# Mixture-of-experts blocks in two parts, with routing, scatter, gather and norm of one part beside the blocks of the other

## The chip, the cores and the metric

The kernel runs on one core of a Trainium2 chip. Its engines run at the same time and meet by semaphores: TensorE (PE; PEld is its weight load), VectorE (DVE), ScalarE (ACT), GpSimd (POOL) and SyncE (SP). The metric is the device time of one execution in microseconds (us), as the median of the runs.

## The reference

The input x is 4 x 1024 x 128 (four batches). Two layers follow each other, each with an attention and a mixture of experts:

```python
for layer in (0, 1):
    sa, ca, ga, sb, cb, gb = mod(c)                  # six vectors of 128 per batch
    h = layernorm(x) * (1 + ca) + sa
    x = x + ga * attention(h)      # layer 0: 16 heads, window 64; layer 1: 16 heads of 8, full
    h = layernorm(x) * (1 + cb) + sb
    x = x + gb * experts(h)
# experts, layer 0 (F = 512; layer 1: F = 256, no biases, tanh gelu, and a small
# attention across the four batches before it)
    xn = layernorm(h) * gamma + beta
    probs = softmax(xn @ Wg.T + bg)                  # 8 experts, for each of 4096 tokens
    w = the two largest of probs (layer 0: over their sum), else 0
    y_e = gelu(xn @ W1[e].T + b1[e]) @ W2[e].T + b2[e]
    out = h + sum_e w[:, e] * y_e
```

Every token thus needs two of eight experts.

## The kernel before

**Stages.** The program is a row of stages, each an `nc.Block` with one instruction list for every engine. At the end of a stage all engines drain and meet, so a stage begins when the slowest engine has ended the last one. Within a stage each list is run in its written order.

**Tiles.** x lies in SBUF as 32 tiles of 128 tokens (NT), 8 to a batch (TPB), and is handled in 8 chunks of 4 tiles (CPT, NCH). K.nat holds the modulated h, K.x the residual stream. `K.mod_rows` holds the modulation vectors on every partition.

**Routing** (class `RoutedExperts`, M). For each batch TensorE makes the logits, and VectorE and ScalarE the softmax and the two choices. `place` gives each token and choice a row number in a DRAM buffer `moe_rows`, a region of 4096 rows for each expert (SPAN = B·T), by a running count over the batches. GpSimd then scatters each normalised tile twice by an indirect DMA, 64 in a layer (`scatter_one`, L1413; `scatter`, L1402). `tabulate` (VectorE, L1378 to L1394) turns the counts into a table: for each of NBK = 39 blocks of 256 rows (2·4096/256 + 8 - 1) its expert and its first row. 39 always suffice, since each of the eight experts fills at most one block in part; the others take spare rows.

**Layer 0's order.** The window attention routes batches 0 to 2 beside its own work, one batch behind. `route_last_stage` (L1102) takes batch 3: both norms, logits, choice, place, table, and on GpSimd the 32 scatters of batches 2 and 3. Then `block_stage` with name moe0b, then `gather_qkv_stage` (L1682), which gathers the experts' rows, sums them into x, and makes norm and q, k, v of layer 1's attention. The attention (its first product L2021) starts behind it.

**Layer 1's order.** `last_norm_stage` (L292, L316) normalises and routes all four batches and scatters 64 times; then `block_stage` as moe1b, then `gather_stage` (L1602), which ends the program with the output stores.

**Block stage** (L1454). For block j SP loads the 256 rows (xin, 6 buffers) and the expert's weights (wblock, 6 buffers). TensorE turns block j+1 (`turn`, xps), makes the hidden layer of block j (hps) and the output rows of block j-1 (yps). VectorE copies xps to xT with the affine (L1556), and yps to y (L1566 with bias, L1568 without). ScalarE issues the store of block j-3 back into `moe_rows` (L1528) and does the gelu (L1542). xps and yps have two PSUM banks each. VectorE adds gb·h to x by two instructions for a chunk (L1578, L1580, `residual`) in blocks 2 to 9. GpSimd only clears operands of the coming attention in layer 0 (L1879), and has nothing in layer 1.

```python
                    if j + 1 < NBK:
                        turn(j + 1)
                    if j < NBK:
                        hidden(j)
                    if j >= 1:
                        out_rows(j - 1)
```

**Gather.** GpSimd gathers two rows for each token, 64 indirect DMAs of a tile each (L1687, L1606). When a chunk's 8 gathers are in, it is multiplied by the first weight (ScalarE in layer 0, L1749; VectorE in layer 1), and VectorE does a fused multiply and add for each tile (L1787), the gate, and the sum into x (L1795). In layer 0, GpSimd's norm step (`deviation`, L145) of a batch stands between the gathers.

## Time and profile before

| | us |
|---|---|
| median of 3 runs | 2082.85 |
| lowest and highest | 2081.83, 2082.87 |
| the profiled execution | 2078.63 |
| its span in the trace | 2076.9 |
| route_last_stage, from the end of the window attention to the first load of the blocks | 617.1 to 679.4 |
| block stage moe0b | 679.4 to 837 |
| gather_qkv_stage up to attention's first product | 837.3 to 957.3 |
| last_norm_stage up to the first load of the blocks | 1784.9 to 1898.3 |
| block stage moe1b | 1898.3 to 1988 |
| gather_stage | 1988.4 to 2076.9 |

TensorE is busy 76% of the span, VectorE 64%, ScalarE 55% and GpSimd 26%. These shares are averages over stages with different limits, so they are read by stretch of the program. The trace gives each instruction's start and length, the time for which its engine was idle before it, and what released it. An engine with a q behind it (SPq, PEq) stands for its queue: DMA issues, drains, branches. The granted clock is TensorE's, 1.00 being 2.4 GHz and 0.50 being 1.2 GHz.

### The profile page before, as it was taken

Reading aid. Unit: us, or ns where it says so; the run is one execution under the profiler, and the core shown is the slowest. Engines: PE = TensorE matmul, PEld = TensorE weight load, DVE = VectorE, ACT = ScalarE, POOL = GpSimd, SP = SyncE. Lnnn points to the kernel's source line nnn. Section 1 sums busy time; section 2 is a strip of 40 time slices with the busy share of each in tenths; the row PEclk is TensorE's granted clock in tenths of the full one; section 3 lists DMA queues with packets and bytes.
Section 4 is the critical chain, followed back from the end, with each engine's and each line's share of the span. In section 5 each row is a group of like instructions: output and inputs, shape, how many; then the busy total and the mean of one; then the engine's idle time right before and its main releaser. Section 6 shows DMA issues by size and latency. Waiting matters only on the chain. (4 is left out here: it accounts for less than half of the span.)

```text
span 2076.9 us, 34430 instructions
## 1 busy us (share of the span) xinstructions
PE 1575.3 (76%) x11512; PEld 915.2 (44%) x11512; DVE 1338.5 (64%) x3318; ACT 1135.4 (55%) x2965; POOL 550.0 (26%) x615
## 2 busy tenths in 40 slices
...
GB/s 189 42 162 157 103 28 35 45 31 40 40 21 41 230 226 183 57 134 63 20 26 18 26 18 26 20 24 25 19 18 2 1 4 0 13 52 123 255 86 73
DMA packets 86203, 138.99 MB, mean 67 GB/s; under 512 B 18084, under 2 KB 57252, under 8 KB 85900
## 3 DMA queue, kind: packets, MB, share of 16 engines
...
## 5 line engine op out<-in xcount | busy, mean ns | idle before, releaser
L2130 DVE TENSOR_REDUCE q_max<-s_ps 128x1 f32<-128x1024 f32 x512 | 597.9, 1217 | 14.6 <-PE s_ps L2021 7.0
L2111 ACT ACTIVATE probs<-s_ps 128x512 f32<-128x512 f32 x1024 | 535.5, 602 | 124.8 <-PE s_ps L2042 124.6
L2021 PE MATMUL s_ps<-k_stack,q_stack 64*128 64x512 bf16 x1024 | 351.8, 397 | 17.5 <-PEq L96 9.1
L2042 PE MATMUL s_ps<-q_stack,k_stack 64*128 64x512 bf16 x1024 | 319.9, 385 | 20.2 <-ACT probs L2111 15.7
L2056 PE MATMUL o_ps<-probs,v_aug 128*32 128x512 f32 x2048 | 273.7, 607 | 0.7 <-ACT probs L2111 0.7
L2042 PEld LDWEIGHTS s_ps<-q_stack,k_stack 64*128 64x128 bf16 x1024 | 78.5, 94 | 334.6 <-ACT probs L2111 282.6
L1058 POOL TENSOR_TENSOR probs<-probs,p_rsum 128x512 f32<-128x512 f32 x128 | 133.1, 1040 | 323.8 <-DVE p_rsum L1035 323.1
L938 ACT ACTIVATE probs<-s_biased,s_min 128x128 f32<-128x128 f32 (+1 forms) x512 | 197.7, 391 | 37.0 <-DVE s_min L1029 35.6
L803 PE MATMUL score_ps<-k_pad,q_bd 128*128 128x128 f32 x1024 | 145.7, 286 | 0.0
L1029 DVE CUSTOM_DVE_ANT_0 s_biased<-score_ps,nbias 128x128 f32<-128x128 f32 (+1 forms) x512 | 115.7, 281 | 40.2 <-PE score_ps L803 38.9
L1648 POOL CAST neg_max_parts<-neg_max 16x128 bf16<-16x128 f32 x32 | 9.0, 281 | 474.9 <-DVE neg_max L2138 474.9
L803 PEld LDWEIGHTS score_ps<-k_pad,q_bd 128*128 128x128 f32 x1024 | 125.0, 192 | 7.4 <-issue 1.0
L2021 PEld LDWEIGHTS s_ps<-k_stack,q_stack 64*128 64x128 bf16 x1024 | 77.3, 94 | 113.5 <-DVE q_max L2130 103.9
L961 DVE TENSOR_SCALAR q_bd<-proj_ps,qscale 64x512 f32<-64x512 f32 x64 | 48.4, 756 | 107.3 <-PE proj_ps L783 104.2
L1542 ACT ACTIVATE moe0b_hid<-moe0b_hps,moe0b_wblock 128x256 f32<-128x256 f32 x156 | 67.0, 474 | 84.1 <-PE moe0b_hps L1497 82.3
L1041 DVE COPY probsT<-probsT_ps 128x512 f32<-128x512 f32 x128 | 86.6, 676 | 36.5 <-PE probsT_ps L814 35.8
L1687 POOL DMA_INDIRECT moe0g_yg<-moe_rows,moe_slot x64 | 66.3, 1036 | 159.5 <-POOLq L96 140.7
L938 ACT ACTIVATION_READ_ACCUMULATOR probs<-s_biased,s_min 128x1 f32 x512 | 98.1, 192 | 0.0
L1606 POOL DMA_INDIRECT moe1g_yg<-moe_rows,moe_slot x64 | 61.1, 955 | 121.0 <-PEq L1601 101.8
L888 ACT ACTIVATE q_bd<-proj_ps,qscale 64x512 f32<-64x512 f32 x64 | 43.7, 683 | 84.3 <-PE proj_ps L783 84.3
L1566 DVE TENSOR_TENSOR moe0b_y<-moe0b_yps,moe0b_wblock 128x256 f32<-128x256 f32 x39 | 16.6, 424 | 100.4 <-PE moe0b_yps L1507 100.4
L829 PE MATMUL o_ps<-probsT,v_shift 128*64 128x64 f32 x1024 | 72.8, 233 | 9.2 <-ACT oT L946 9.1
...
## 6 DMA issues: line engine op xcount, KB each, us to landing
...
```

The costliest lines, as they stand in the source:

```text
L803: m = nc.tensor.matmul(sp_[g % 2][:, i, :], qbd[:, h % 2, j, :], kk[:, h % 2, BLK * j:BLK * j + P], start=True, stop=True)
L829: m = nc.tensor.matmul(op[a * BLK:(a + 1) * BLK, i, :], src[:, a * HD0:(a + 1) * HD0], pt[:, k % 2, i, a * BLK:(a + 1) * BLK], start=True, ...
L938: r = nc.scalar.activation(pr[:, g % 3, i, own], sb_[:, g % 2, i, own], ACT.Exp, scale=-1.0, bias=mn[:, g % 4, i:i + 1], accum_out=sm[:, g ...
L1029: q = v.tensor_tensor_reduce(sb_[:, g % 2, i, own], sp_[g % 2][:, i, own], nbias[:, h % PAIRS, own], 1.0, 3e38, ALU.add, ALU.min, mn[:, g ...
L1041: v.tensor_copy(pt[:, k % 2], tp[:]).then_inc(pt_out, 1)
L1058: nc.gpsimd.tensor_tensor(pb, pb, bc(ri[:, g % 4, :], 2, P), ALU.mult).then_inc(normed, 1)
L1542: nc.scalar.activation(hid[:, j % 2, f, :], hp[n % 4][:, 0:BR], gelu, bias=bias).then_inc(g_out, 1)
L2021: mm = nc.tensor.matmul(s1[u % 2][:, c * CH:(c + 1) * CH], qs[head_rows(m), quad % 4, j, qt * P:(qt + 1) * P], ks[head_rows(m), quad % 4, ...
L2042: nc.tensor.matmul(bank_of("exp", 4 * k + pos)[:], ks[head_rows(m), quad % 4, j, kt * P:(kt + 1) * P], qs[head_rows(m), quad % 4, j, half ...
L2056: m = nc.tensor.matmul(op[32 * h:32 * h + 32, :], va[:, quad % 2, kt, h, :], pr[:, k % 2, h, :], start=(kt == 0), stop=(kt == TPB - 1))
L2111: nc.scalar.activation(pr[:, k % 2, HEADS[pos], :], bank_of("exp", n)[:], ACT.Exp).then_inc(sm["exp"], 1)
L2130: v.tensor_reduce(mx[:, h % 4, col:col + 1], s1[u % 2][:], AX.X, ALU.max).then_inc(sm["maxed"], 1)
```

## The change

**Two parts.** The experts of a layer work on batches 0 and 1 (part 0), then on batches 2 and 3 (part 1), each in a block stage of its own: moe0b and moe0c, moe1b and moe1c. A part has its own regions in `moe_rows` (PROWS = 18176 rows each) and its own table of NBK = 23 blocks. `tabulate(part)` for part 0 now runs inside the window attention (layer 0) and after batch 1 in `last_norm_stage` (layer 1).

**Beside work.** `block_stage` takes an object whose `vector(j)`, `tensor(j)` and `scalar(j)` put pieces at the end of step j on those engines, and whose `gpsimd` is GpSimd's whole list in that stage:
- moe0b has `RouteBeside`, what `route_last_stage` did: on TensorE at steps 5, 7 and 11 the 8 transposes, 8 logit products and 2 prefix products of batch 3, on VectorE and ScalarE its norms, choice, place and table, and the scatters of batches 2 and 3. `route_last_stage` is gone.
- moe0c has `GatherBeside` (moe0h): the 32 gathers of batches 0 and 1, their products on ScalarE, their sums on VectorE, the norm of layer 1 for these batches, and then the clears that stood in moe0b.
- moe1b has `ScatterBeside`: the 32 scatters of batches 2 and 3; `last_norm_stage` keeps those of 0 and 1.
- moe1c has `GatherBeside` (moe1h) without the norm; GpSimd then issues the four output stores of these batches.

The separate gather stages keep batches 2 and 3. xps and yps go from two PSUM banks to one each, so `turn(j)` waits for xT of block j-1 and `out_rows(j)` for y of j-1. The residual pieces stand at steps 17 to 20, four in each part. `mod_rows` holds four of six vectors (from GA on), and 19 fills clear `moe_rows`, not 18.

```diff
-SPAN = B * T
-NBK = 2 * B * T // BR + E - 1
+HB = B // 2
+SPAN = HB * T
+NBK = 2 * SPAN // BR + E - 1
...
+class RouteBeside:
+    def vector(self, dve, j):
+        if j == 0:
+            N1.statistics(dve, b)
+        elif j == 1:
+            N1.normalised_odd(dve, b)
+        elif j == 2:
+            N1.wait_normalised(dve, NT)
...
+        elif j == 3:
+            dve.wait_ge(self.shifted, 1)
+            N2.statistics(dve, b)
+        elif j == 4:
+            N2.normalised_odd(dve, b)
+        elif j == 8:
+            M.shift_logits(dve, b, self.raw_logits)
+        elif j == 9:
+            M.probabilities(dve, b)
+            M.compare(dve)
+        elif j == 10:
+            M.order(dve)
+        elif j == 11:
+            M.weights(dve, b)
+        elif j == 12:
+            M.place(dve, b, self.prior)
+        elif j == 13:
+            M.tabulate(dve, 1)
+    def tensor(self, pe, j):
+        if j == 5:
+            N2.wait_normalised(pe, NT)
...
+        elif j == 7:
+            pe.wait_ge(self.turn_out, 2)
...
+        elif j == 11:
+            pe.wait_ge(M.chose, b + 1)
...
+    def scalar(self, act, j):
+        if j == 1:
+            self.N1.normalised_even(act, b)
+        elif j == 4:
+            self.N2.normalised_even(act, b)
+        elif j == 6:
+            for i in range(2):
+                act.wait_ge(self.turned, i + 1)
...
+        elif j == 9:
+            M.exponentials(act, b)
+        elif j == 12:
+            act.wait_ge(M.prefixed, b + 1)
...
+    def gpsimd(self, pool):
+        N1.deviation(pool, b)
+        for n in range(11):
+            M.scatter_one(pool, N2, b - 1, n)
+        N2.deviation(pool, b)
+        for n in range(11, 2 * TPB):
+            M.scatter_one(pool, N2, b - 1, n)
+        for n in range(2 * TPB):
+            M.scatter_one(pool, N2, b, n)
+        M.wait_scattered(pool, B)
...
+class ScatterBeside:
+    def gpsimd(self, pool):
+        for b in range(HB, B):
+            self.M.scatter(pool, self.N, b, 0, TPB)
+        self.M.wait_scattered(pool, B)
...
+class GatherBeside:
+    PRODUCTS = {3: 0, 5: 1, 9: 2, 11: 3}
+    SUMS = {4: 0, 6: 1, 10: 2, 12: 3}
+    def vector(self, dve, j):
+        if j in self.SUMS:
+            c = self.SUMS[j]
+            for t in range(c * CPT, (c + 1) * CPT):
+                dve.wait_ge(self.first, t + 1)
+                v.scalar_tensor_tensor(out=yg[:, t, 0, :], in0=yg[:, t, 1, :], scalar=M.weight[:, 1, t:t + 1],
+                                       in1=yg[:, t, 0, :], op0=ALU.mult, op1=ALU.add).then_inc(self.summed, 1)
...
+            v.tensor_tensor(K.x[:, ts, :], K.x[:, ts, :], yg[:, ts, 0, :], ALU.add).then_inc(self.added, 1)
+        if self.N is not None:
+            if j in (7, 13):
+                b = (7, 13).index(j)
+                dve.wait_ge(self.added, 2 * b + 2)
+                self.N.statistics(dve, b)
+            if j in (9, 15):
+                self.N.normalised_odd(dve, (9, 15).index(j))
+    def scalar(self, act, j):
+        if j in self.PRODUCTS:
+            c = self.PRODUCTS[j]
+            act.wait_ge(self.got[c], 16 * 2 * CPT)
...
+        if self.N is not None and j in (10, 16):
+            self.N.normalised_even(act, (10, 16).index(j))
+    def gpsimd(self, pool):
+        self.gather(0, 3 * TPB)
+        if self.N is not None:
+            self.N.deviation(pool, 0)
+        self.gather(3 * TPB, 4 * TPB)
+        self.last(pool, self)
...
-        xp = [K.ps(f"{name}_xps{i}", [P, CH], st) for i in range(2)]
+        xp = K.ps(name + "_xps", [P, CH], st)
...
-                    if j >= 2:
-                        pe.wait_ge(x_out, j - 1)
+                    if j >= 1:
+                        pe.wait_ge(x_out, j)
...
-                    if j >= 2:
-                        pe.wait_ge(y_out, j - 1)
+                    if j >= 1:
+                        pe.wait_ge(y_out, j)
...
-                    if 2 <= j < NCH + 2:
-                        residual(j - 2)
+                    if NBK - 6 <= j < NBK - 6 + NCH // 2:
+                        residual(j - (NBK - 6))
+                    beside.vector(dve, j)
```

**GpSimd, layer 1, from the routing to the end.** Before, all scatters stand in the routing stage, the block stage has no instruction of GpSimd, and all gathers follow. The branches mark the stages' ends.

```order
L145 TENSOR_TENSOR n1d_rstd<-n1d_ve,neghalf 128x8 x4
L1402 DMA moe_rows<-n1d_hat,moe_slot 34560x128 x64
L292 UNCONDITIONAL_BRANCH
L95 ISA x4
L1602 UNCONDITIONAL_BRANCH
L1606 DMA moe1g_yg<-moe_rows,moe_slot 128x128 x64
```

Of the change:

```order
L1537 DMA moe_rows<-n1d_hat,moe_slot 36480x128 x32
L291 UNCONDITIONAL_BRANCH
L97 ISA
L1591 UNCONDITIONAL_BRANCH
L1537 DMA moe_rows<-n1d_hat,moe_slot 36480x128 x32
L1590 UNCONDITIONAL_BRANCH
L97 ISA x3
L1591 UNCONDITIONAL_BRANCH
L1247 DMA moe1h_yg<-moe_rows,moe_slot 128x128 x32
L1785 DMA out_x<-x 128x4x128 x4
...
L1745 DMA moe1g_yg<-moe_rows,moe_slot 128x128 x32
```

Half of the scatters stand in the first block stage, half of the gathers and four stores in the second, and 32 gathers are left behind them.

**VectorE, layer 1, early block steps.** Before, a residual piece (gx, x) stands in each step from the third on; xT and y are the block's own two.

```order
L1556 TENSOR_SCALAR moe1b_xT<-moe1b_xps,moe_affine 128x256
L1568 COPY moe1b_y<-moe1b_yps 128x256
L1578 TENSOR_TENSOR moe1b_gx<-nat,mod_rows 128x512
L1580 TENSOR_TENSOR x<-x,moe1b_gx 128x512
L1556 TENSOR_SCALAR moe1b_xT<-moe1b_xps,moe_affine 128x256
L1568 COPY moe1b_y<-moe1b_yps 128x256
```

Of the change, in moe1c, steps 4 and 5:

```order
L1693 TENSOR_SCALAR moe1c_xT<-moe1c_xps,moe_affine 128x256
L1705 COPY moe1c_y<-moe1c_yps 128x256
L1258 SCALAR_TENSOR_TENSOR moe1h_yg<-moe1h_yg,moe_weight 128x128 x4
L1263 TENSOR_TENSOR moe1h_yg<-moe1h_yg,mod_rows 128x4x128
L1265 TENSOR_TENSOR x<-x,moe1h_yg 128x512
L1693 TENSOR_SCALAR moe1c_xT<-moe1c_xps,moe_affine 128x256
```

The sum of a chunk, six instructions, now stands between the y of one block and the xT of the next but one; it waits for ScalarE's products.

**ScalarE, layer 0, step 9 of moe0b.** Before, the exponential stood in `route_last_stage`, with one table load ahead of the gelus:

```order
L1289 ACTIVATE moe_ex<-moe_lg 128x64
L1366 COPY moe_totals<-moe_counts_ps 128x8x8
L1102 UNCONDITIONAL_BRANCH
L1521 UNCONDITIONAL_BRANCH
L1428 TENSOR_LOAD moe_table
L1428 ISA x8
L1542 ACT_TABLE_LOAD
L1542 ACTIVATE moe0b_hid<-moe0b_hps,moe0b_wblock 128x256 x12
```

Of the change:

```order
L1678 ACTIVATE moe0b_hid<-moe0b_hps,moe0b_wblock 128x256 x4
L1423 ACT_TABLE_LOAD
L1423 ACTIVATE moe_ex<-moe_lg 128x64
L1664 ISA
L1664 DMA moe_rows<-moe0b_y 128x256
L1678 ACT_TABLE_LOAD
L1678 ACTIVATE moe0b_hid<-moe0b_hps,moe0b_wblock 128x256 x4
```

It stands between the gelus of two blocks, and two table loads with it.

## Rows read from the trace of the kernel before

**Rows 1.** Busy time of the engines by stretch of the program (columns in the first row)

```profile
core 0: us, PE busy (x) PEld busy (x) DVE busy (x) ACT busy (x) POOL busy (x), PEclk, DMA share, GB/s
598.00:679.00 81.00, 21.44 (x214) 18.62 (x210) 33.50 (x140) 15.47 (x54) 42.73 (x41) 0.63 0.08 27
679.00:837.00 158.00, 149.16 (x1014) 139.66 (x1014) 44.77 (x94) 66.98 (x157) 17.19 (x9) 0.96 0.68 212
837.00:957.00 120.00, 35.32 (x128) 21.82 (x128) 67.21 (x194) 42.36 (x88) 73.33 (x68) 0.63 0.35 103
1780.00:1898.00 118.00, 26.49 (x112) 23.69 (x112) 41.88 (x180) 15.40 (x33) 69.63 (x68) 0.50 0.12 37
1898.00:1988.00 90.00, 81.37 (x546) 74.37 (x546) 44.50 (x94) 28.73 (x78) 0.00 (x0) 0.96 0.73 229
1988.00:2077.00 89.00, 0.00 (x0) 0.00 (x0) 26.47 (x80) 0.00 (x0) 61.12 (x64) 0.50 0.27 71
```

**Rows 2.** Timeline, layer-0 block: start, us, engine, line, work, [idle before <-releaser]

```profile
745.54 0.38 PE L1486 MATMUL moe0b_xps<-ident,moe0b_xin 128*128 128x128 f32 x2
...
746.08 0.53 DVE L1556 TENSOR_SCALAR moe0b_xT<-moe0b_xps,moe_affine 128x256 f32<-128x256 f32 x1
...
749.27 0.38 PE L1486 MATMUL moe0b_xps<-ident,moe0b_xin 128*128 128x128 f32 x2
```

**Rows 3.** The y tiles: duration ns min/median/max, first to last start

```profile
L1566 DVE TENSOR_TENSOR moe0b_y<-moe0b_yps,moe0b_wblock x39: 423/425/426, 693.5 to 833.1; 128x256 f32<-128x256 f32 x39
L1568 DVE COPY moe1b_y<-moe1b_yps x39: 414/425/426, 1907.3 to 1984.3; 128x256 f32<-128x256 f32 x39
```

**Rows 4.** The indirect DMAs as issued by GpSimd, columns as in 3

```profile
L1402 POOL DMA_INDIRECT moe_rows<-n1d_hat,moe_slot x64: 954/958/1473, 1804.5 to 1885.6; - x64
L1687 POOL DMA_INDIRECT moe0g_yg<-moe_rows,moe_slot x64: 940/948/1622, 837.3 to 926.3; - x64
L1606 POOL DMA_INDIRECT moe1g_yg<-moe_rows,moe_slot x64: 940/945/1143, 1988.4 to 2067.7; - x64
```

**Rows 5.** Timeline, end of window attention and first load of the blocks

```profile
615.85 1.29 DVE L1015 TENSOR_TENSOR x<-x,wo_ps 128x512 f32<-128x512 f32 x2 [3.69 <-PE wo_ps L842]
...
679.40 0.36 SPq L1469 DMA_DIRECT2D moe0b_xin<-moe_rows  x1
```

**Rows 6.** Drains that end layer 1's routing, and the first load behind

```profile
L292 DVEq DRAIN  x1: 271/271/271, 1833.3 to 1833.3; - x1
L292 POOLq DRAIN  x1: 5271/5271/5271, 1888.0 to 1888.0; - x1
...
1898.29 0.35 SPq L1469 DMA_DIRECT2D moe1b_xin<-moe_rows  x1
```

**Rows 7.** Timeline, first product of the layer-1 attention

```profile
957.33 1.04 PE L2021 MATMUL s_ps<-k_stack,q_stack 64*128 64x512 bf16 x4 [9.10 <-PEq L96]
```

**Rows 8.** Timeline, first and last step of the table, a table load, a chunk's sums

```profile
649.16 0.16 DVE L1378 TENSOR_TENSOR moe_nb<-moe_cum,moe_steps 128x8 f32<-128x8 f32 x1
...
653.76 0.20 DVE L1394 CAST moe_table<-moe_tf 128x78 int32<-128x78 f32 x1
...
677.74 1.28 ACT L1542 ACT_TABLE_LOAD   x1 [30.47 <-issue]
...
883.09 1.13 DVE L1787 SCALAR_TENSOR_TENSOR moe0g_yg<-moe0g_yg,moe_weight 128x128 f32<-128x128 f32 x4
...
884.97 0.69 DVE L1795 TENSOR_TENSOR x<-x,moe0g_yg 128x512 f32<-128x512 f32 x1
```

**Rows 9.** Busy time in four short stretches, columns as in 1

```profile
1850.00:1886.00 36.00, 0.00 (x0) 0.00 (x0) 0.00 (x0) 0.00 (x0) 27.24 (x29) 0.50 0.16 53
1940.00:1960.00 20.00, 20.00 (x144) 18.97 (x144) 8.76 (x20) 7.45 (x21) 0.00 (x0) 1.00 0.83 265
688.00:690.00 2.00, 2.00 (x7) 1.53 (x7) 0.54 (x1) 0.87 (x2) 1.94 (x2) 0.50 1.08 337
692.00:694.00 2.00, 2.00 (x19) 1.95 (x18) 0.50 (x2) 0.19 (x1) 2.00 (x1) 1.00 0.88 349
```

375 lines of the change are left out of this document (204 added, 171 removed).

## Prediction

> **What bounds the kernel now.** I read the busy times by stage first, since the share of a whole span says nothing about a stage [rows 1]. Six stretches matter. In the two block stages (679 to 837, 1898 to 1988) TensorE is busy 149 of 158 us and 81 of 90 at nearly full clock: these are bound by TensorE. In the four others TensorE is mostly idle (0 to 35 us busy): 598 to 679 and 1780 to 1898 are routing and scatter, 837 to 957 and 1988 to 2077 are gather. There GpSimd is the busy engine, and it issues indirect DMAs in a row: 64 scatters from 1804.5 to 1885.6, 64 gathers from 837.3 to 926.3 and 64 from 1988.4 to 2067.7 [rows 4]. That is one per 1.29, 1.41 and 1.26 us, and each batch takes 16. While GpSimd works TensorE waits, and while TensorE works GpSimd waits (0.00 busy in 1898 to 1988). So there is something to overlap, and the question is what the overlap costs.
>
> **What one block stage of 23 takes.** 39 blocks become 23 twice, 46, since every part pads its own eight experts: 7 more blocks per layer. Layer 0: the first y is written at 693.5, the last at 833.1 [rows 3], 38 intervals in 139.6; in mid-stage one takes 3.73 (transposes at 745.54 and 749.27) [rows 2], so the tail saves 2.1. The first load is issued at 679.40 [rows 5], 14.1 before the first y; that ramp runs at clock 0.50 with saturated transfers [rows 9]. A stage of 23: 14.1 + 22 x 3.73 - 2.1 + 0.4 = 94.5 us. Layer 1: first load 1898.29 [rows 6], first y 1907.3, then 77.0 / 38 = 2.03 [rows 3]: 9.0 + 22 x 2.03 + 0.4 = 54 us. I assume the ramp for each of the four stages. From the last y to the next stage's first GpSimd instruction are 3.75 us (833.55 to 837.3) [rows 3, 4]; from the end of a GpSimd drain to the first load 5.0 (1893.3 to 1898.3) [rows 6]. Last y to first load is then between 3.75 and 8.8; I take 7.
>
> **Layer 0, routing to the blocks.** The window attention ends at 617.1 [rows 5]. Its table of part 0 is now worked out inside it, a chain of 4.8 us on VectorE (649.16 to 653.96) [rows 8]; attention keeps several groups in flight, so I charge 2 (bounds 0 and 5). Plus 5 to the first load: 624 instead of 679.4. The stage is 94.5 plus what stands beside it:
> - TensorE has no free time: 8 transposes, 8 logit products and 2 prefix products at some 0.19 us (two transposes in 0.38) [rows 2] are 3.4.
> - VectorE has room. Between y (0.42) and xT (0.53) a block of 3.73 leaves about 2.7 us [rows 2, 3]; a piece up to that length is hidden by TensorE's block. Statistics, norm, modulation and comparison are each near or under it; the table, 4.8, is over by 2.
> - ScalarE is busy 67 of 158 [rows 1], so 2 us a block are free. One exponential between Gelus brings two more table loads of 1.28 [rows 8], and ScalarE waits once for the norm: 1 + 1.
> - GpSimd scatters batches 2 and 3, 32 x 1.27 = 41 us. Batch 3 can start only after block 12, near 65 us into the stage, and is over some 22 later (16 x 1.29 and the landing) [rows 4]; the stage has 102, so 15 are spare.
> In all 8 (bounds 3 and 19, where nothing fits): 624 + 94.5 + 8 = 726.5. With 7, the second stage loads at 733.5. Its gathers are hidden; the queue halts at GpSimd's norm step until block 7, so chunk 3 arrives near 787 where block 11 would take it at 785. With rest 3: 733.5 + 94.5 + 3 = 831, and the gather stage starts at 834.8 instead of 837.3.
> **Layer 0, gather stage.** 26 + 6 gathers instead of 64: 31 x 1.41 = 43.8, then the tail as before, from the last gather at 926.3 to attention's first product at 957.3 [rows 4, 7], 31.0. Sum 74.8 instead of 120.0: 45.2. VectorE's work (67 busy before, [rows 1]) falls only to some 54, hence this can't shrink below about 70. With the 2.5: **47.7 us** gained.
>
> **Layer 1.** The 32nd scatter is issued at 1804.5 + 31 x 1.29 = 1844.4; from the last scatter to the first load are 12.7 as before (5.3 of it the drain [rows 6]): 1857.1. VectorE's chain, which ended at 1833.3 [rows 6], gets one more table of 4.8 and ends near 1838, still ahead of the scatters. + 54 = 1911.1; the other 32 scatters take 41 + 12 of these 54 us, so they just fit. + 7: 1918.1. The stage of part 1 pays three things:
> - a sum of a chunk is 2.6 us on VectorE (883.09 to 885.66) [rows 8], while a block of 2.03 leaves 1.1. Since xT now has to leave the only bank before the next transposes, TensorE waits 1.5 to 1.7 for each: 4 x 1.7 = 7.
> - chunk 3 is there 31 x 1.26 + 2.6 = 41.7 after the first gather, at 1956.6; ScalarE asks for it near 1952 (y 10 at 1947.4 and 5 us of delays). With the products: 5.
> - the four out stores of part 0 go by GpSimd's queue and hide.
> 1918.1 + 54 + 12 = 1984.1, + 3.75: the last gather stage starts at 1987.9 instead of 1988.4. It has 32 gathers fewer, 32 x 1.26 = 40.3. Together **40.8 us**.
> **Transfers.** The layer-1 blocks hold the 16 DMA engines 0.83 busy, a scatter queue alone 0.16; the loads at 688 to 690 reach 1.08 at 337 GB/s [rows 9]. The sum of 0.99 is just under what has been seen, with no room for bursts. Bounds 0 and, if only 0.9 are had in steady state, 0.2 us for each of 40 blocks plus late chunks, 11. I take 5: the rows show the full rate. Layer 0 moves less per us and is inside it.
> The smaller mod_rows load is beside ScalarE's work at the start, and 19 clears instead of 18 lie beside attention: nothing.
>
> **The sum.** 47.7 + 40.8 - 5 = 83.5. In each layer the block stages eat up what they hide, and what is left is the shorter gather stage. The profiled execution took 2078.63 (span 2076.9), so it would be 1995; the median of the runs shown is 4.2 higher: 2082.85 - 84 = **1999 us**.
>
> **Rivals.**
> (A) As summed: 1990 to 2010. 54%.
> (B) The cover leaks: transfers at their upper bound (+6), pieces on VectorE that don't fit (+11 in layer 0, some in layer 1), which gives 2016 (2010 to 2030). For it: 0.99 of the DMA engines, one bank instead of two for xps and yps, 1.1 us of room in layer 1. Against it: the room of 2.7 us in layer 0. 25%.
> (C) Less is lost: the clock is still high when block stages follow each other or attention (0.50 in the ramp of layer 0, 1.00 four us later) [rows 9], the ramp is 3 to 4 us shorter three times, transfers cost nothing: 1986 (1975 to 1990). 14%.
> (D) On the other side: GpSimd's indirect DMAs slow down beside VectorE. Those of the layer-0 gather, with VectorE busy 67 of 120 us, had a median of 0.948 us (longest 1.6); those of layer 1, with 26 of 89, had 0.945 (longest 1.1) [rows 1, 4]. So the busier VectorE made no difference to the median, which speaks against it. If each waited for a whole VectorE instruction and the step became 2.5 us, 32 would need 80: chunk 3 comes 38 late in both gather-beside stages, layer 1's scatters end 27 after their blocks, layer 0's some 3: 106 us, so 2105. It turns the sign from a step of about 2.2 us. 4%.
> The Trainium skill, "SBUF — State Buffer", section on who interferes with whom, says that a DMA of the GpSimd queue starves while VectorE runs a 2-port copy, cast or tensor_scalar from SBUF to SBUF, because the descriptors can't be written, and advises against hiding such DMAs under VectorE. By its conditions the block's own two VectorE steps read PSUM and tensor_tensor has no such mode; only the norm's steps and the routing's small ones would count, which is a few us and inside (A). Read without its conditions it is (D).
> (E) The stalls let TensorE's clock fall to its lower level, 1.2 GHz, and the blocks run at half speed as in 688 to 690 [rows 9]. A layer-0 block would then cost 3.7 more; 23 of them eat the whole gain, all 23 of one stage give about 2084. Stages that let TensorE idle for tens of us did show 0.5 to 0.63 [rows 1]; the stalls here are 2 to 5 us between long runs. 3%.
>
> **Chances.** What a measurement of this kernel can tell from no change is about 0.2%, 4 us. Cases A, B and C lie below all of it: 93%, and a mild D or E 1% more: faster 0.94, same 0.01, slower 0.05. The range holds A, B and the upper part of C: 1984 to 2030.
>
> **What would show it.** First load of the first block stage near 624 and of layer 1 near 1857; four block stages of 102, 97, 54 and 66 us; first gather of the separate stages near 835 and, in the old kernel's time, 1988; 32 gathers in each, tails 31 and 9. If the layer-1 stage beside the gathers is much over 66, see whether TensorE waits for xT (pieces), for xin (transfers) or ScalarE for chunk 3. Wrong would be the sum if a scatter or gather steps at over 1.5 us, if the granted clock in the block stages is under 0.9, or if attention does not begin 48 us earlier.

## The result

The changed kernel takes 2115.64 us (median of 4 runs, 2112.91 to 2120.32) where the kernel before takes 2082.49: a ratio of 1.016 with an interval of 1.0148 to 1.0173. The forecast was 1999, in a range of 1984 to 2030. It is slower by 1.6%, clear of the noise: 33 us more where 84 less were expected. The profiled execution took 2118.16, of which the span is 2116.3.

### The profile page after: what moved, and what is told of

Its sections match the earlier page's. It is cut to its first block and busy times, and to the rows that moved or that the text cites. A ratio compares the mean times of both kernels' runs of the same rounds, so it can differ in the third digit from the quotient of the medians.

```text
span 2116.3 us, 35460 instructions
## 1 busy us (share of the span) xinstructions
PE 1646.2 (78%) x11792; PEld 972.3 (46%) x11792; DVE 1357.7 (64%) x3360; ACT 1157.6 (55%) x3025; POOL 547.7 (26%) x620
## 3 DMA queue, kind: packets, MB, share of 16 engines
q8 instruction: 96, 1.57, 0.3%
## 5 line engine op out<-in xcount | busy, mean ns | idle before, releaser
L1044 DVE COPY probsT<-probsT_ps 128x512 f32<-128x512 f32 x128 | 86.6, 677 | 35.9 <-PE probsT_ps L815 35.2
L1678 ACT ACTIVATE moe0c_hid<-moe0c_hps,moe0c_wblock 128x256 f32<-128x256 f32 x92 | 39.9, 473 | 86.5 <-PE moe0c_hps L1632 42.1
L815 PE MATMUL probsT_ps<-ident,probs 128*128 128x128 f32 x512 | 77.9, 275 | 4.6 <-POOL probs L1061 4.6
L815 PEld LDWEIGHTS probsT_ps<-ident,probs 128*128 128x128 f32 x512 | 62.1, 142 | 37.8 <-issue 31.6
L1548 POOL DMA_INDIRECT moe_rows<-hk,moe_slot x64 | 66.7, 1042 | 43.4 <-DVE moe_slot L1494 28.8
```

Source lines behind the costliest of these rows:

```text
L815: m = nc.tensor.transpose(tp[:, i, :], pr[:, k % 3, i, :], K.ident[:])
L1044: v.tensor_copy(pt[:, k % 2], tp[:]).then_inc(pt_out, 1)
```

## The profile after

First the busy times by stretch, the columns as in [rows 1]: the two block stages of layer 0, the gather stage up to attention, the two block stages of layer 1, the last gather stage.

```profile
core 0: us, PE busy (x) PEld busy (x) DVE busy (x) ACT busy (x) POOL busy (x), PEclk, DMA share, GB/s
624.00:746.00 122.00, 99.15 (x626) 89.79 (x626) 45.79 (x141) 46.08 (x106) 34.26 (x34) 0.89 0.56 178
754.00:880.00 126.00, 98.93 (x598) 89.36 (x598) 46.87 (x122) 47.58 (x116) 51.80 (x42) 0.84 0.55 172
884.00:977.00 93.00, 35.77 (x130) 22.00 (x132) 49.80 (x126) 34.01 (x65) 34.99 (x34) 0.67 0.36 111
1875.00:1962.00 87.00, 53.38 (x322) 47.62 (x322) 25.60 (x54) 16.92 (x46) 28.72 (x30) 0.77 0.51 161
1969.00:2064.00 95.00, 55.59 (x322) 48.66 (x322) 35.34 (x78) 21.81 (x62) 31.49 (x35) 0.77 0.54 159
2067.00:2116.00 49.00, 0.00 (x0) 0.00 (x0) 13.22 (x40) 0.00 (x0) 30.55 (x32) 0.50 0.24 64
```

In [rows 1] TensorE was busy 149 of 158 us and 81 of 90 in the block stages. Now it is 99 of 122, 99 of 126, 53 of 87 and 56 of 95. So all four block stages lost what bounded them. Their y tiles give the lengths (duration ns min/median/max, first to last start; the rows of before are [rows 3]):

```profile
L1703 DVE TENSOR_TENSOR moe0b_y<-moe0b_yps,moe0b_wblock x23: 424/425/426, 637.2 to 745.4; 128x256 f32<-128x256 f32 x23
L1703 DVE TENSOR_TENSOR moe0c_y<-moe0c_yps,moe0c_wblock x23: 407/424/425, 785.5 to 879.4; 128x256 f32<-128x256 f32 x23
L1705 DVE COPY moe1b_y<-moe1b_yps x23: 412/424/425, 1892.3 to 1961.1; 128x256 f32<-128x256 f32 x23
L1705 DVE COPY moe1c_y<-moe1c_yps x23: 412/425/425, 1988.0 to 2063.1; 128x256 f32<-128x256 f32 x23
```

Set against the terms of the sum (from first load to the end of the last y; the last column is the fastest kernel of the study, best7, which comes below):

| | forecast | changed kernel | best7 |
|---|---|---|---|
| first load of moe0b | 624 | 623.8 | 624.2 |
| moe0b | 102.5 | 122.0 | 99.9 |
| moe0c | 97.5 | 126.0 | 99.0 |
| layer-0 gather stage to attention | 74.8 | 92.7 | 79.5 |
| attention to first load of moe1b | 899.8 | 898.2 | 899.0 |
| moe1b | 54 | 86.6 | 54.7 |
| moe1c | 66 | 94.5 | 62.0 |
| last gather stage | 48.2 | 48.6 | 48.4 |

The loss sits in five stages: 19.5 + 28.5 + 17.9 + 32.6 + 28.5 = 127 us. The rest of the sum holds to 2 us a term, so no other large mistake hides in it. And 127 less the 5 allowed for transfers is 122, within 1 us of what lies between the forecast for this execution, 1995, and its 2118.

**What such a stretch looks like.** This is the timeline of moe0b, 639 to 651 us (start, length, engine, line, work, idle time before and its releaser):

```profile
638.96 1.95 PE L1642 MATMUL moe0b_yps<-moe0b_wblock,moe0b_hid 128*128 128x128 f32 x16
...
640.96 1.89 PE L1632 MATMUL moe0b_hps<-moe0b_xT,moe0b_wblock 128*128 128x256 f32 x8
...
641.64 0.96 POOL L1548 DMA_INDIRECT moe_rows<-hk,moe_slot  x1 [0.30 <-issue]
...
646.70 0.95 POOL L1548 DMA_INDIRECT moe_rows<-hk,moe_slot  x1 [0.30 <-issue]
649.55 0.42 DVE L1703 TENSOR_TENSOR moe0b_y<-moe0b_yps,moe0b_wblock 128x256 f32<-128x256 f32 x1 [10.36 <-DMA v_shift<-v_tiles]
649.70 1.57 ACT L1678 ACTIVATE moe0b_hid<-moe0b_hps,moe0b_wblock 128x256 f32<-128x256 f32 x4 [8.18 <-remote]
```

TensorE's products for y end at 640.9, those of the next hidden layer at 642.85. VectorE needs only the first to write y, and ScalarE only the second for its gelu. Both wait until 649.6. The releasers printed are no help: the DMA named had ended long ago. What stands in the gap is GpSimd, with one scatter after the other in 1.26 us, the last at 646.70. Nothing else happens on any engine, and then all go on within 0.6 us. Four such stretches, in the columns of the first fence:

```profile
642.60:649.60 7.00, 0.26 (x2) 0.00 (x0) 0.05 (x1) 0.00 (x0) 3.83 (x4) 0.88 0.15 52
704.00:716.00 12.00, 5.36 (x24) 3.31 (x24) 0.54 (x1) 1.42 (x3) 7.30 (x8) 0.72 0.35 106
767.20:785.50 18.30, 3.65 (x10) 1.50 (x8) 0.00 (x0) 1.41 (x3) 10.85 (x12) 0.60 0.43 131
1999.00:2011.50 12.50, 0.00 (x0) 0.00 (x0) 0.00 (x0) 0.38 (x1) 5.69 (x7) 0.50 0.37 101
```

TensorE does 0.3, 5.4, 3.7 and 0.0 us of work in them, VectorE 0.05, 0.54, 0 and 0, while GpSimd starts 4, 7, 11 and 6 indirect DMAs (three of the counts hold the end of one more). The DMA engines are busy 0.15 to 0.43 in them, against 0.56 over the whole of moe0b, so it is not the DMA engines that are full. In the layer-0 gather stage the same happens with no block beside it at all. TensorE turns a batch's second chunk, and ScalarE's copy of it waits for 22 us, until the row of 26 gathers (884.0 to 915.6) is over:

```profile
897.50 1.04 PE L179 MATMUL n1a_ps<-ident,nat 128*128 128x128 f32 x8
920.58 1.45 ACT L186 ACTIVATE hT<-n1a_ps,mod_cols 128x512 f32<-128x512 f32 x2 [18.64 <-remote]
921.41 2.92 PE L1878 MATMUL qk_ps<-hT,w_qkvT 128*128 128x512 f32 x3 [22.87 <-ACT hT L186]
```

SyncE gives the second sign. L1563 (L1428 before) are the instructions in which it loads and checks the addresses of the next four blocks, on its own registers. The rows show the same code in the changed kernel and before:

```profile
L1563 SPq FUSED_REGOPS  x184: 3/147/712, 621.2 to 2048.1; - x184
L1428 SPq FUSED_REGOPS  x156: 147/147/187, 676.8 to 1970.6; - x156
```

A register operation of SyncE, 147 ns before and never over 187, takes up to 712 ns, and a check of 18 ns up to 709. GpSimd itself is not slowed: its gathers in moe1c had a median of 944 ns, as in [rows 4].

```profile
L1247 POOL DMA_INDIRECT moe1h_yg<-moe_rows,moe_slot x32: 940/944/976, 1966.8 to 2005.6; - x32
```

## The experiments

From this came the theory, called R on record: a row of back-to-back indirect DMAs on GpSimd holds up what TensorE tells the others, and SyncE. (probe1 and probe2, at the end, widened "what TensorE tells" to every engine's instructions.) Its rivals were T (loads and gathers compete for the DMA engines) and P (the pieces on VectorE and ScalarE and the single PSUM banks cost it). The kernel before was run again beside them. It took 2082.85 beside run8, run4 and bursts, 2087.64 beside pace640, pace192, spaced and split1, 2087.19 beside sizes, best384 and best288, 2087.3 beside unpaced and best7, 2084.29 beside probe1 and 2081.61 beside probe2. Only best384, best288 and best7 were run more than once (4, 4 and 5 times).

### run8 and run4: shorter rows

```diff
+RUN = 8
...
+            if n and n % RUN == 0:
+                self.nc.gpsimd.wait_ge(self.got[(n - 1) // 8], 16 * ((n - 1) % 8 + 1))
             self.nc.gpsimd.indirect_dma_start(
                 self.yg[:, t, c, :], None, self.K.moe_rows,
```

and so for the scatters and the layer-0 gather stage; run4 has RUN = 4.

> The changed kernel, with one edit: in the two block stages with scatters, the two with gathers and in layer 0's gather stage, GpSimd waits after every 8 indirect DMAs until they have landed; all work is kept. Theory R (a long row of back-to-back indirect DMAs on GpSimd holds up what TensorE tells the others and each instruction of SyncE, from about the 8th or 10th DMA of the row to some 4 us behind its last; the changed kernel loses about 20 us in each of moe0b, moe0c and the layer-0 gather stage, and 30 in each of moe1b and moe1c): the stalls go, about 120 us less, of which the added waits of some 2.5 us, three for each 32 DMAs, give back 5 to 20: 1998 to 2030. Theory T (the loads and the gathers compete for the DMA engines): the same bytes go in about the same time, so 2105 to 2120. Theory P (the pieces on VectorE and ScalarE and the single PSUM banks cost it): 2110 to 2125, since GpSimd's work only gets longer.

> As run8, with the wait after every 4 indirect DMAs. Theory R: if rows of 8 are short enough, this is worse than run8, by four more waits of 2.5 us for each 32 DMAs where GpSimd's row ends last (moe1b, moe1c): run8 + 10 to 25. If rows of 8 still stall, this is better than run8. T and P: no better than the changed kernel's 2116.

Measured: run8 2073.03, run4 2046.02. T and P had both at 2105 or more, since waits were only added, and they fall with that. R had the sign right, its size wrong: rows of 8 still stalled, rows of 4 nearly not. So "from the 8th or 10th DMA on" was too narrow.

### bursts: spare DMAs beside the blocks of the kernel before

```diff
+    def one(self, indirect=True):
+        dst = self.got[:, self.slot, :]
+        if indirect:
+            self.nc.gpsimd.indirect_dma_start(
+                dst, None, self.src, bass.IndirectOffsetOnAxis(ap=self.idx[:, 0:1], axis=0)).then_inc(self.landed, 16)
+        else:
+            self.nc.gpsimd.dma_start(dst, self.src[self.slot * P:(self.slot + 1) * P, :]).then_inc(self.landed, 16)
```

> The kernel before, with rows of 64 KB that GpSimd reads from x into a spare tile while the blocks run; they change nothing of what is computed. In moe0b, behind the clears: indirect DMAs in rows of 6, 10 and 16, each followed by its landing and some 6 us of memsets, then 3 rows of 8 with 1 to 2 us between them. In moe1b: 24 plain DMAs of the same size in a row, then 20 indirect ones with a memset of some 0.7 us behind each. Theory R: the rows of 6 and 10 cost nothing or up to 3 us, the row of 16 costs 8 to 14 us, and the blocks pass the rest undisturbed if a short pause is enough; if it is not, the rows of 8 cost another 10 to 20. If the matter is indirect DMAs, the 24 plain ones cost nothing; if it is any DMA from GpSimd, 15 to 25. The spaced ones tell whether it is the rate (no stall) or the count (10 to 25). Sum: 2095 to 2140. T: each row costs in proportion to its bytes, with no stretch in which TensorE stands still for 5 us or more: 2085 to 2100. P says nothing on it: 2083.

Measured: 2126.74, 44 us over the kernel before beside it. The stretches of moe0b with the rows of 6, 10, 16 and three times 8, and one without any:

```profile
702.00:717.00 15.00, 13.34 (x96) 12.48 (x95) 6.82 (x14) 5.18 (x13) 11.31 (x15) 1.00 0.69 229
717.00:738.00 21.00, 16.15 (x92) 14.42 (x92) 6.89 (x14) 6.93 (x16) 15.64 (x21) 0.86 0.61 195
738.00:765.00 27.00, 17.39 (x94) 14.24 (x94) 3.29 (x8) 5.29 (x12) 20.41 (x25) 0.79 0.46 142
765.00:806.00 41.00, 28.95 (x154) 23.06 (x153) 4.69 (x11) 10.66 (x24) 27.34 (x32) 0.92 0.49 148
806.00:840.00 34.00, 34.00 (x239) 32.12 (x238) 8.19 (x19) 15.39 (x36) 0.00 (x0) 1.00 0.78 246
```

The counts of TensorE's products price each row. Undisturbed it does 239 in 34 us, 7.03 a us. In 717 to 738 it would do 147.6 and does 92, so 55.6 / 7.03 = 7.9 us are lost by ten DMAs, where R had 3 at most. The same for the others gives 1.3 us for the row of 6, 13.6 for 16 and 19.1 for the 24 in rows of 8. Together 42, and from first to last y it is 182.6 instead of 139.6 [rows 3], 43.0. Some 1 to 2 us of pause between rows of 8 don't help.

The block stage of layer 1 had 24 plain DMAs of the same 64 KB each, issued every 0.53 us from 1941.7 to 1954.4, most of it in the ramp, and then 20 indirect ones with a memset of 128x640 behind each, at a step of 1.87 us:

```profile
L1538 SPq DMA_DIRECT2D moe1b_xin<-moe_rows x39: 4/333/355, 1941.8 to 2018.4; - x39
L1637 DVE COPY moe1b_y<-moe1b_yps x39: 415/424/426, 1951.9 to 2028.0; 128x256 f32<-128x256 f32 x39
```

From first load to last y these are 86.2 us (1941.8 to 2028.0), against 86.0 before (1898.3 to 1984.3) [rows 3, 6]. So neither plain DMAs nor spaced indirect ones cost anything. (The plain ones meet dense work only at their end, but indirect ones in the same place do hurt: in the run sizes, below, the ramp beside 24 of them took 21.8 us, 1957.9 to 1979.7, where it is 10.1 here.) That is the row that split R in two: R1, the step decides, and R2, the count in a row decides.

### pace640, pace192 and spaced: the step

```diff
+class Pace:
+    def __call__(self):
+        if self.width:
+            self.nc.gpsimd.memset(self.pad[:], 0.0).then_inc(self.done, 1)
+            self.n += 1
+            self.nc.gpsimd.wait_ge(self.done, self.n)
```

In the changed kernel it is called behind each indirect DMA that has TensorE's work beside it; spaced does the same with the spare DMAs of bursts.

> The changed kernel with a memset of 128x640 on GpSimd behind each indirect DMA of the four block stages and of layer 0's gather stage, so that they step at 1.87 us, as the spaced row in moe1b of the run bursts did without a stall. Theory R1 (it is the rate: somewhere between 1.25 and 1.87 us a step GpSimd's indirect DMAs begin to hold up TensorE's completions and SyncE, how long the row is only sets how long it lasts): no interval of blocks over 8 us that is not a wait for a gathered chunk, moe0b about 20 us shorter than in the changed kernel; but 32 of them take 60 us instead of 41, so moe1b is 18 longer than its 54, moe1c 24 longer than its 66, the layer-0 gather stage 15 longer than 75, moe0c 8 longer: 1995 + 65 = 2060 (2045 to 2070). Theory R2 (it is the count in a row, and only a pause until they have landed clears it): stalls as in the changed kernel, 2115 to 2140.

> As pace640 with a memset of 128x192, a step of about 1.45 us. R1: if the limit lies under 1.45 us, no stalls and less lateness than pace640: 2010 to 2035. If it lies above, stalls of a length between those of the changed kernel and none: 2060 to 2100. R2: 2115 to 2130.

> The kernel before with spare indirect DMAs of 64 KB on GpSimd beside the blocks, as in the run bursts, now all spaced: in moe0b 20 with a memset of 128x384 behind each, 20 with 128x192, 16 with 128x64; in moe1b 16 with 384, 16 with 192. R1: the loss for one DMA falls with the step, from some 0.77 us at 1.25 (56 of them cost 43 us in the run bursts) to 0 at 1.87; with a drain of fixed rate r it is the step that is missing to r, so at r = 1.6 rows of 384 (about 1.6) cost 0, of 192 (1.45) 3 us, of 64 (1.3) 5 us. R2: each row of 16 to 20 costs 10 to 17 us whatever its step.

Measured: pace640 2057.74, pace192 2043.95, spaced 2116.88 (kernel before 2087.64). R2 is out: pace640 has 24 and 32 in a row and no stall of that kind, and it came within 3 us of what R1 gave. Its remaining losses are GpSimd's own lateness, 32 DMAs in 60 us. pace192 fell between R1's two ranges (2010 to 2035 without stalls, 2060 to 2100 with them): its scatters in layer 1 stepped at 1.51 us, and moe1b took 69 us instead of 54, so it still stalls, and gives part of it back by being less late. In spaced, rows of 20 with 128x384 (1.66 us), 20 with 128x192 (1.5 us) and 16 with 128x64 (1.39 us by 20.8 us for 15 steps) in moe0b:

```profile
702.00:736.00 34.00, 34.00 (x240) 32.14 (x239) 15.68 (x30) 15.38 (x36) 28.84 (x40) 1.00 0.80 262
745.00:783.00 38.00, 34.99 (x214) 31.58 (x213) 7.11 (x16) 14.45 (x35) 30.05 (x50) 0.91 0.69 218
783.00:812.00 29.00, 20.60 (x122) 17.23 (x121) 3.60 (x8) 7.42 (x18) 22.53 (x41) 0.88 0.59 183
```

In the first TensorE is busy all 34 us and does its 240 products. In the others 53 and 82 are missing, 7.6 and 11.7 us. The drain of fixed rate on record (3 and 5 us) is out with that. In layer 1 of the same run 16 DMAs with 128x384 left the steps of the blocks as before, and 16 with 128x192 (1957.8 to 1981.1) made 25.5 us out of seven of them, which are 14 undisturbed: 11.5 lost. With bursts, the loss for one indirect DMA against its step is:

| step, us | row | us lost for one |
|---|---|---|
| 1.25 | 10, 16 or 8 + 8 + 8 | 0.79 to 0.85 |
| 1.25 | 6 | 0.2 |
| 1.39 | 16 | 0.73 |
| 1.50 | 20 | 0.38 |
| 1.50 (layer 1) | 16 | 0.72 |
| 1.66 | 20 | 0 |
| 1.66 (layer 1) | 16 | 0 |
| 1.87 (layer 1) | 20 | 0 |

So the limit lies between 1.5 and 1.66 us. It is no gentle cost: at 1.39 more time is lost than if each DMA had been put off to 1.66.

### sizes: bytes or rows of a DMA

```diff
+    def one(self, indirect=True, rows=P, cols=D):
+        dst = self.got[0:rows, self.slot, 0:cols]
```

> The kernel before with spare indirect DMAs back to back beside the blocks: in moe0b 24 of 128 rows of 128 bytes instead of 512, then 24 of 64 rows of 512 bytes; in moe1b 24 of 64 rows, then 16 of 128 rows as in the changed kernel. If it is the bytes moved, the first two rows cost nothing and the last 10 to 12 us. If it is the descriptors (one for each row), the 24 of 128 short rows cost as full ones, some 0.77 us each or 18, and those of 64 rows next to nothing, unless their step is half as long too. Plain DMAs of the same bytes at a step of 0.6 us cost nothing in the run bursts, which speaks for descriptors.

Measured: 2181.22, 94 us over the kernel before. The stretches in moe0b with 24 DMAs of 128 rows of 128 bytes, and with 24 of 64 rows of 512 bytes:

```profile
700.00:738.00 38.00, 20.21 (x97) 16.17 (x96) 7.67 (x16) 5.29 (x13) 28.78 (x33) 0.65 0.28 86
738.00:785.00 47.00, 28.93 (x130) 23.92 (x129) 8.45 (x17) 8.96 (x20) 27.89 (x34) 0.66 0.34 111
```

Of 267 and 330 products 97 and 130 are done: 24.2 and 28.5 us are lost, 1.0 and 1.2 us for one. Both guesses on record fall. Neither a quarter of the bytes nor half of the rows makes it cheaper, and the steps are nearly the same (1.25 and 1.20 us). In layer 1, 24 of 64 rows and then 16 whole ones made the block stage 38 us longer, 0.95 us for one. So the price goes with the number and step of the indirect DMAs. Why it is 1.0 to 1.2 here and 0.8 in bursts isn't shown; the rows are longer, so less of each is free.

### split1: the split without anything beside it

```diff
-                for b in range(HB):
+                for b in range(B):
                     M.scatter(pool, N, b, 0, TPB)
...
     def gpsimd(self, pool):
-        for b in range(HB, B):
-            self.M.scatter(pool, self.N, b, 0, TPB)
-        self.M.wait_scattered(pool, B)
+        pass
```

moe1c has the same empty helper, and the last stage gathers all 64.

> The changed kernel, with layer 1 in two parts but GpSimd idle beside them: all 64 scatters stand ahead of moe1b and all 64 gathers behind moe1c, as in the kernel before. It prices the split alone. The prediction's terms for it: 23 blocks 54 us, 7 us between the stages, 23 blocks 54 us, against 86 us for 39; layer 1 then takes 29 us more than before, and layer 0 is that of the changed kernel, 19 more than before: 2079 + 19 + 29 = 2127 (2122 to 2132). Theory R (1 or 2): neither moe1b nor moe1c has a stall; their blocks step at 2.0 us in spite of single PSUM banks. Theory P (single banks): steps of 2.3 or more.

Measured: 2136.04, beside 2087.64 for the kernel before. Layer 1's two stages:

```profile
L1602 SPq DMA_DIRECT2D moe1b_xin<-moe_rows x23: 332/333/354, 1920.9 to 1962.7; - x23
L1703 DVE COPY moe1b_y<-moe1b_yps x23: 416/425/425, 1930.4 to 1975.6; 128x256 f32<-128x256 f32 x23
L1602 SPq DMA_DIRECT2D moe1c_xin<-moe_rows x23: 332/333/800, 1982.8 to 2024.2; - x23
L1703 DVE COPY moe1c_y<-moe1c_yps x23: 415/425/426, 1992.1 to 2036.8; 128x256 f32<-128x256 f32 x23
```

From first load to the end of the last y 55.1 and 54.4 us, with 6.8 between, where the forecast had 54, 54 and 7. The total is 9 above what was expected, of which the kernel before beside it has 5. This settles P for the banks: 22 intervals in 45.2 and 44.7 us are 2.05 and 2.03, as with two banks. And a split without an overlap costs what the forecast's lengths say: 1920.9 to 2037.2 are 116.3 us, where 39 blocks in one stage took 86.4 (1898.3 to 1984.7) [rows 3, 6]. That is 30 more; 54 + 7 + 54 gives 29.

### best384 and best288: the pace that is just enough

```diff
+PACE0, PACE1, PACEQ = 384, 384, 192
...
-    PRODUCTS = {3: 0, 5: 1, 9: 2, 11: 3}
-    SUMS = {4: 0, 6: 1, 10: 2, 12: 3}
+    PRODUCTS_OF = ({3: 0, 5: 1, 9: 2, 12: 3}, {4: 0, 10: 1, 16: 2, 22: 3})
+    SUMS_OF = ({4: 0, 6: 1, 10: 2, 13: 3}, {5: 0, 11: 1, 17: 2, 23: 3})
...
-BEFORE_DEV = 10
+BEFORE_DEV = 6
```

> The changed kernel with a memset of 128x384 on GpSimd behind each indirect DMA of the block stages (a step of about 1.66 us, at which the run spaced lost nothing) and one of 128x192 behind the first 16 gathers of layer 0's gather stage, GpSimd's norm step there after 6 gathers of the next batch instead of 10, and products and sums at later blocks: in moe1c products at 4, 10, 16, 22 and sums at 5, 11, 17, 23, since a chunk of 8 gathers now lands each 13 us, in moe0c the last chunk and its norm one block later. Theory R1 (GpSimd's indirect DMAs hold up the others when they step faster than some 1.5 to 1.6 us): no stall, stages of about 102, 100, 58, 64 us and a gather stage of 77 from its first gather to attention: 2003 (1995 to 2020). R2 (count in a row): over 2090. If something else in the block stages costs, as single banks or pieces, it comes out between 2025 and 2060.

> As best384 with memsets of 128x288 in the block stages, a step of about 1.57 us. R1 with a limit under 1.57: 4 to 8 us faster than best384 (moe1b and moe1c end with GpSimd's row). With a limit between 1.57 and 1.66: 5 to 25 slower, by stalls in all four stages.

Measured: best384 2009.79 (ratio 0.9631, interval 0.9614 to 0.9648), best288 2011.65 (0.9632, 0.9615 to 0.9650), the kernel before 2087.19. The forecast of 2003 was meant for a chip on which the kernel before takes 2083; on this one it takes 4 more. The two can't be told apart, where 4 to 8 us less or 5 to 25 more had been expected. At 1.57 us the shorter rows of GpSimd and a few stalls (two intervals of 3.0 and 4.1 us in moe1c where best384 has 2.0) may cancel.

### unpaced and best7: what did it, and the last wait

unpaced is best384 with `PACE0, PACE1, PACEQ = 0, 0, 0`. best7 is best384 with:

```diff
-        for n in range(11):
+        for n in range(7):
             M.scatter_one(pool, N2, b - 1, n)
         N2.deviation(pool, b)
-        for n in range(11, 2 * TPB):
+        for n in range(7, 2 * TPB):
```

> best384 without any of its memsets, so GpSimd's indirect DMAs step at 1.25 us again; the later products and sums and the earlier norm step of the gather stage stay. Theory R1 (the step is what matters): the stalls are back, 2090 to 2115, at most 15 better than the changed kernel by the schedule. If the schedule is what won, and not the step: 2000 to 2025.

> best384 with GpSimd's second norm step of batch 3 in moe0b after 7 scatters of batch 2 instead of 11. In best384 it stands from 647.3, when VectorE has its statistics, to 653.8 behind four paced scatters, and the two block intervals around it last 9.1 and 7.7 us instead of 3.7. R1 has nothing to say on it; by the queue it should save 5 us: 2004 (2001 to 2008). If ScalarE's own place for the norm is what holds it, nothing: 2009.

Measured: unpaced 2126.48, best7 2003.15 (2001.55 to 2005.57, 5 runs; ratio 0.9602, interval 0.9586 to 0.9617), beside 2087.3 for the kernel before. unpaced lies above its range of 2090 to 2115. The later schedule alone is worth nothing, and is even 11 us worse than the changed kernel's median, of which the kernel before beside it accounts for 5. 144 memsets of 0.43 us or less, with a wait for each, make it 117 us faster. best7 is 6.6 us under best384, where 5 had been read from the queue. Its stages, in the order of the first fence without the last:

```profile
624.00:724.00 100.00, 92.88 (x626) 86.37 (x626) 46.80 (x141) 46.45 (x106) 48.25 (x66) 0.95 0.68 217
733.00:832.00 99.00, 89.47 (x598) 83.13 (x598) 46.79 (x122) 47.09 (x116) 66.04 (x74) 0.94 0.67 219
838.00:917.50 79.50, 32.45 (x129) 20.23 (x131) 49.99 (x126) 33.44 (x65) 40.42 (x50) 0.69 0.42 130
1816.50:1871.00 54.50, 49.98 (x322) 45.33 (x322) 25.23 (x54) 16.90 (x46) 43.81 (x62) 0.91 0.79 258
1878.00:1941.00 63.00, 51.62 (x322) 46.63 (x322) 33.31 (x75) 21.46 (x62) 46.29 (x65) 0.90 0.75 236
```

TensorE is busy 93 of 100 us, 89 of 99, 50 of 54.5 and 52 of 63, with the clock at 0.90 to 0.95 instead of 0.77 to 0.89.

### probe1 and probe2: what a stall needs

Behind the kernel before, short stages of their own. GpSimd's part is the same in all, and the rest is one of three patterns:

```diff
+    def products(self, name, count, width, groups, dmas, loads=0, out=False, ints=0):
...
+                    for g in range(groups):
+                        if g >= 2:
+                            pe.wait_ge(copied, g - 1)
+                        for i in range(count):
+                            m = nc.tensor.matmul(bank[g % 2][:, 0:width], K.ident[:], rows[:, 0:width],
+                                                 start=True, stop=True)
+                        m.then_inc(filled, 1)
```

> The kernel before, and behind its last gather stage eight short stages, whose results go nowhere. In each GpSimd issues 28 indirect DMAs back to back (step 1.25 us, 35 us; pa: none), TensorE fills two banks in turn and ScalarE copies 32 columns of each. pa and pb: 24 groups of 16 products of 128x128 by 128x128; pc: 24 groups of 2 by 128x512; pd: 60 groups of 1 by 128x128; pe: one group of 384 without a wait; pf: as pb with 32 plain loads of 128 KB on SyncE; ph: 48 groups of 8. pg has no TensorE work: VectorE and ScalarE copy 128x64 to each other, 60 times. Open is what a stall needs beside the row: in the kernel before a row of 22 scatters (1804.5 to 1832) has TensorE's results reach ScalarE 0.03 us after their end, at some 3 products a us. Theory N (number of TensorE's instructions): products and weight loads pile up something that drains slowly beside the row. pb lasts 20 us or more longer than pa, pf and ph alike, pc (1.2 products a us), pd and pg end as if undisturbed. Theory L (the block stage's plain loads and stores are needed): pb, pc, pd, ph as pa; only pf longer. Theory W (every wait for TensorE behind the 6th DMA is hit): pb, pc and pd lose 0.8 us for each DMA issued meanwhile; pg nothing. Theory A (any engine's signal): pg lasts longer too. If pe's products end at their usual pace and its copy comes late, TensorE isn't held up, only its signal is.

> As probe1, with other short stages behind the kernel before. What probe1 left open: one product for each wait (pd) lost as much as 16, and yet the kernel before has 22 scatters beside routing steps without delay. qa, qb, qc do what the routing does, one thing at a time: 14 products, a copy of ScalarE, 20 dependent copies of 128x64 on VectorE, 9 times; qa without, qb with 28 gathers, qc with 28 scatters in a row. qd and qe: 24 groups of 16 products beside 28 gathers (as pb, which took 115.6 us against 88.5) and 28 scatters. qf and qg: VectorE alone, 200 dependent copies, without and with 28 gathers. qh: as qd, the row 8 us later. Theory S (a scatter is cheaper than a gather): qe loses under 15 us, qd 27 as pb; qc as qa, qb longer by 10 or more. Theory D (how much the engines do in a time): qe as qd, 27; qb and qc both within 3 us of qa; qg loses little, under 3. Theory C (any work beside the 8th DMA of a row is held up): qb and qc both 15 us or more over qa, qg as well. In theory D the routing rows of the kernel before were free because little else ran.

Measured, from the start of the first instruction to that of the last (the two kernels whole: 2802.14 and 2858.46):

| stage | beside 28 indirect DMAs | us | without |
|---|---|---|---|
| pb, qd | 24 groups of 16 products, gathers | 115.6, 116.1 | 88.5 (pa) |
| qe | the same, scatters | 113.6 | 88.5 |
| pf | the same, with 4 MB of plain loads | 116.8 | 88.5 |
| ph | 48 groups of 8 | 117.6 | 88.5 |
| pe | 384 products, no wait in them | 114.2 | 88.5 |
| qh | as qd, row 8 us later | 116.9 | 88.5 |
| qb, qc | one thing at a time, gathers and scatters | 108.3, 108.3 | 93.0 (qa) |
| qg | VectorE alone | 61.9 | 45.6 (qf) |

pc, pd and pg have no stage without DMAs beside them. pd did 41 recorded products in its first 10 us and 18 in the next 25, pc 24 in its first 10 and 12 in the 17 from 2312 on; so both were held up. Of the theories, N, L and W of probe1 fall, and S and D of probe2: scatters and gathers are alike, plain traffic adds 1 us, and work of one thing at a time loses 15 us where D allowed 3. A stands: every engine is held up, VectorE alone too. C (any work beside the 8th DMA) fits the losses of all probes, but not the kernel before, as the next section shows. And pe shows that it isn't the signals: with no wait inside, TensorE lost 26 us. So the first reading of the timeline of moe0b was too narrow. This is the timeline of VectorE in qg, columns as above:

```profile
2674.77 20.22 DVE L2544 COPY qg_a<-qg_a 128x64 f32<-128x64 f32 x81
...
2704.09 0.20 DVE L2544 COPY qg_a<-qg_a 128x64 f32<-128x64 f32 x1 [0.34 <-DVE qg_a L2544]
2705.49 0.20 DVE L2544 COPY qg_a<-qg_a 128x64 f32<-128x64 f32 x1 [1.21 <-DVE qg_a L2544]
```

And this the busy time in three stretches of pb, columns as in [rows 1]:

```profile
2180.00:2190.00 10.00, 7.30 (x59) 6.50 (x58) 0.00 (x0) 0.18 (x1) 7.56 (x9) 1.00 0.19 54
2200.00:2211.00 11.00, 1.69 (x5) 1.44 (x5) 0.00 (x0) 0.00 (x0) 8.04 (x9) 0.50 0.18 51
2220.00:2250.00 30.00, 30.00 (x266) 30.00 (x266) 0.00 (x0) 1.48 (x8) 0.00 (x0) 0.98 0.00 1
```

For 20 us VectorE does 81 copies beside 16 gathers, nearly as if alone (81 / 200 of 45.6 us are 18.5). Then one copy of 0.20 us is done in 0.7 or 1.4 us, the same 0.7 us as SyncE's 709 and 712 ns. In pb TensorE goes undisturbed for about 10 us, 8 DMAs, then comes down to 5 recorded products in 11 us, and is back at full pace (266 in 30 us) 9 us behind the row. So the 0.8 us for one DMA is a mean over a free start and a rest in which nearly everything stops. Why the routing of the kernel before, with 22 scatters in a row and work like qc's, stays free while qc doesn't is open.

## Why the prediction was wrong

- **What bounds the kernel.** Right: GpSimd's rows and TensorE's blocks took turns, and overlapped they give 84 us, as best7 shows: 2087.3 - 2003.2. That this is the forecast's 84 to the us is partly luck: in best7 the gather stage took 4.7 more than forecast (79.5) and moe1c 4.0 less, and its later schedule was not part of the change.
- **Stage lengths.** 94.5 and 54 us for 23 blocks, 7 between stages, 7 blocks more for a layer: right, by split1 and by best7 (99.9, 99.0, 54.7, 62.0 with what stands beside them).
- **VectorE's and ScalarE's pieces, single banks.** Right in size. A chunk's sum in layer 1 makes two intervals of 3.3 and 2.4 us out of two of 2.0, 1.7 together, and undisturbed intervals are 3.73 and 1.98 with one bank.
- **"In all 8", "its gathers are hidden", "they just fit", "31 x 1.41".** This is the step that failed, in all five stages at once. GpSimd's rows were costed by their own length and set against the length of the blocks, at a price of nothing for the others. They cost the other engines about 0.8 us for each indirect DMA. 154 of them now stood beside other engines' work (4 x 32 and 26), and 154 x 0.8 is 123 us, where the five stages lost 127. It is a mean: by stage it is 0.6 to 1.0 (19.5 us for 32 in moe0b, 32.6 for 32 in moe1b).
- **Rival (D)** had the right instruction and the wrong direction. It let VectorE slow GpSimd's DMAs, priced that by the median of [rows 4], which was unmoved, and gave it 4%. It was unmoved now too, 944 ns. The page of the Trainium skill that it named, "SBUF — State Buffer" on who interferes with whom, warns that such DMAs starve beside VectorE. The rows here show single ones of up to 1.6 us [rows 4], but a median that stays; the page's advice, not to hide them there, would have given the right sign by another mechanism than the one measured.
- **What the rows before could have told.** The total of the cost was not in them, and what they had pointed the wrong way. In layer 1's routing 22 scatters stand in a row beside products, with no delay before the 18th, and the table's chain behind it takes the 4.8 us of [rows 8]. And in the last gather stage 64 gathers stand in a row at a step of 1.26 us [rows 4] beside the sums of VectorE, some 70 instructions in 80 us, and VectorE is idle as long before a chunk's sum at about the 57th gather as at the 18th (the trace of before, columns as in the timeline above):

```profile
1826.40 0.63 PE L1264 MATMUL moe_counts_ps<-moe_chosen,moe_ones 128*128 128x64 f32 x2
1827.07 0.21 ACT L1366 COPY moe_totals<-moe_counts_ps 128x64 f32<-128x64 f32 x1 [5.40 <-PE moe_counts_ps L1264]
1827.44 1.02 POOL L1402 DMA_INDIRECT moe_rows<-n1d_hat,moe_slot  x1 [0.30 <-issue]
...
2009.90 0.96 DVE L1619 TENSOR_SCALAR moe1g_u<-moe1g_yg,moe_weight 128x128 f32<-128x128 f32 x4 [6.67 <-DMA moe1g_yg<-moe_rows,moe_slot]
...
2060.23 0.91 DVE L1619 TENSOR_SCALAR moe1g_u<-moe1g_yg,moe_weight 128x128 f32<-128x128 f32 x4 [6.71 <-DMA moe1g_yg<-moe_rows,moe_slot]
```

  And in the gather stage of layer 0, TensorE's work of each batch (the first from 873.5 to 882.4) comes behind a norm step of GpSimd, which breaks the row. So a row's price also depends on how much stands beside it, and with little it is nothing. None of these rows has dense work beside it for long. That row was missing, so the price should have had the whole length of the rows as its upper end: 154 x 1.27 = 196 us, which would have carried the range past 2083.
- **Rivals (B), (C), (E).** Transfers are no term: best7's layer-1 stages need 54.7 and 62.0 with the DMA engines at 0.79 and 0.75. The clock did fall, to 0.77 in layer 1, but as a result of the stalls.

What stays open is what GpSimd's indirect DMAs share with every engine's instructions, why a row is free for its first 8 to 16, and how much work beside it is too much: the routing row of 22 was free to its end, the gather row of 64 too, and the chain of qc was not. The runs show that it hangs on the step and on what runs beside, not on bytes, row count, direction or plain traffic. Every timed execution here left a recorded span and clock, so the runs can't tell whether the recording of instructions has a part in it. And nothing between 1.50 and 1.57 us or between 1.57 and 1.66 was tried.
